# A fixed-point exponential on VectorE and a bias tile in ScalarE's exponentials, in a differential-attention block

## What is computed

```python
scores = jnp.einsum('bhtd,bhsd->bhts', q, k)          # 32 maps of 2048x2048 for each batch
attn_w = jax.nn.softmax(scores.astype(jnp.float32), axis=-1)
aw = attn_w.reshape(Bsz, H, 2, Tt, Tt)
aw = aw[:, :, 0] - lam * aw[:, :, 1]
attn = jnp.einsum('bhts,bhsd->bhtd', aw, v)
```

## Time and profile before

| what | value |
|---|---|
| median of 3 runs | 3668.96 us (3667.09 to 3672.54) |
| time of the profiled execution | 3665.59 us |
| its span, first to last instruction | 3663.9 us |
| mean granted TensorE clock | 0.986 |
| ScalarE busy | 3516.9 us, 96% |
| TensorE busy | 3381.3 us, 92% |
| VectorE busy | 2854.8 us, 78% |
| exponentials on ScalarE | 2732 instructions, 3479.8 us |

### The profile page before, as it was taken

The page is one execution under the profiler, slowest core; times in us unless marked ns, Lnnn a source line. Parts: engine busy times, 40 slices in busy tenths (PEclk is TensorE's granted clock), DMA queues, the critical chain, the costliest instruction groups (busy, mean ns, idle before and its releaser), DMA issues. The chain is left out here.

```text
span 3663.9 us, 74558 instructions
## 1 busy us (share of the span) xinstructions
PE 3381.3 (92%) x30574; PEld 754.8 (21%) x30574; DVE 2854.8 (78%) x4024; ACT 3516.9 (96%) x2808; POOL 449.9 (12%) x283
## 2 busy tenths in 40 slices
PE   8898989999899999999989999999998999989998
PEld 5121111122121121212212112121221111111112
DVE  6688888884598888888368888888747778878876
ACT  4999999999999999999999999999999999999997
POOL 3111101020010111111001110111101001000001
PEclk9999999999999999999999999999999999999999
DMA  6111110111111111111121111111012111000011
GB/s 193 37 27 44 32 36 21 34 43 33 43 39 28 44 50 40 42 29 50 41 48 42 34 36 50 45 42 53 29 35 63 47 36 31 22 27 21 20 27 32
DMA packets 221201, 150.94 MB, mean 41 GB/s; under 512 B 127420, under 2 KB 206220, under 8 KB 220844
## 3 DMA queue, kind: packets, MB, share of 16 engines
q1 hardware_dynamic: 220028, 145.19, 14.9%
q10 hardware_dynamic: 816, 0.79, 0.1%
HBM read 72.50 MB, written 59.19 MB: 36 GB/s over the span
## 5 line engine op out<-in xcount | busy, mean ns | idle before, releaser
L1229 ACT ACTIVATE probs<-ps 128x1536 f32<-128x1536 f32 (+1 forms) x2732 | 3479.8, 1628 | 88.1 <-PE ps L1344 83.1
L1372 PE MATMUL ps<-probs,values 128*32 128x512 f32 x14492 | 2067.4, 610 | 55.5 <-DVE wmod_sb L1721 42.6
L1344 PE MATMUL ps<-queries,keys 25*128 25x512 f16 x7680 | 1008.2, 388 | 184.0 <-ACT probs L1229 161.1
L1344 PEld LDWEIGHTS ps<-queries,keys 25*128 25x128 f16 x7680 | 248.9, 91 | 2024.9 <-ACT probs L1229 1907.6
L1372 PEld LDWEIGHTS ps<-probs,values 128*32 128x32 f32 x14492 | 301.4, 108 | 477.9 <-issue 417.0
L1151 POOL TENSOR_TENSOR seg_rs<-seg_ms,neg_half 128x16 f32<-128x16 f32 x64 | 191.5, 2992 | 1142.0 <-DVE seg_ms L1800 1141.9
L1788 DVE STREAM_TRANSPOSE seg_t<-ps 128x512 f32<-128x512 f32 x127 | 91.0, 717 | 282.3 <-PE ps L1372 281.8
L1717 DVE SCALAR_TENSOR_TENSOR wmod_sb<-wmod_sb 128x1024 f32<-128x1024 f32 x231 | 282.8, 1224 | 5.8
L1699 DVE TENSOR_SCALAR d_y<-ps 128x512 f32<-128x512 f32 x240 | 165.7, 691 | 119.8 <-PE ps L1344 104.9
L1699 DVE TENSOR_SCALAR g_y<-ps 128x512 f32<-128x512 f32 x222 | 153.4, 691 | 120.8 <-PE ps L1344 117.4
L1372 PE MATMUL ps<-wmod_sb,values 128*32 128x512 f32 x868 | 238.7, 630 | 0.0
(11 more groups left out here) (186 smaller groups left out, 1975.2 us busy)
## 6 DMA issues: line engine op xcount, KB each, us to landing
v_scr<-a_v SPq DMA_DIRECT2D x16, 1024.0 KB, 5.0
values<-v_scr SPq DMA_DIRECT2D x29, 512.0 KB
queries<-q_scr SPq DMA_DIRECT2D x116, 96.0 KB
keys<-k_scr SPq DMA_DIRECT2D x116, 96.0 KB
e_x<-in_x_dram SPq DMA_DIRECT2D x18, 512.0 KB, 5.9
attn_scr<-seg_o SPq DMA_DIRECT2D x254, 32.0 KB
e_attn<-attn_scr SPq DMA_DIRECT2D x31, 256.0 KB, 3.7
e_hT<-turned SPq DMA_DIRECT2D x240, 32.0 KB, 2.0
```

What stands on the lines that cost most here:

```text
L1229: nc.scalar.activation(probs[:, s % PRING, at, :], ps[:, base + at.start:base + at.stop:at.step, :], ACT.Exp, scale=1.0 / SQUARE).then_inc ...
L1344: last = nc.tensor.matmul(ps[:, score_bank(n), :], keys[buf][at, u * P:(u + 1) * P], queries[buf][at, tc * CH:(tc + 1) * CH], start=True, ...
L1372: last = nc.tensor.matmul(pv[row:row + VW, :], values[buf][:, n % SEG_BANKS // HEADS, j // 2, :], probs_of(n), start=(i == 0), stop=(i == ...
```

## The change

In `share_part` the seven instructions become six. The score is scaled in `share_read` by log2(e) times 2^23 and written as a 32-bit integer, so that its bits read as a floating-point number hold the whole exponent in the exponent field and the fraction in the mantissa. Two TENSOR_SCALAR instructions with a bitwise AND and an XOR or OR take these two apart, and four SCALAR_TENSOR_TENSOR instructions evaluate a polynomial of degree 6 and multiply. A subtraction (TENSOR_TENSOR) and the rounding and conversion by arithmetic are gone. The blocks of VectorE come out eight times as large as before, and ScalarE's Exp gets a bias of log 8, held in a new tile `eight` of 128x1, so that all exponentials have the same factor. GpSimd writes this tile at the start. The planned costs are those of the six instructions.

```diff
-    D_LINKS = 6
+    D_LINKS = 5
-    SHARE_COST = (695, 1230, 695, 1225, 1225, 1225, 1225)
+    SHARE_COST = (695, 695, 1225, 1225, 1225, 1225)
+            nc.gpsimd.memset(eight[:, :], EIGHT).then_inc(eight_set, 1)
+            act.wait_ge(eight_set, 1)
-                nc.scalar.activation(probs[...], ps[...], ACT.Exp, scale=1.0 / SQUARE).then_inc(exp_done, 1)
+                nc.scalar.activation(probs[...], ps[...], ACT.Exp, bias=eight[:, 0:1], scale=1.0 / SQUARE).then_inc(exp_done, 1)
-                V.tensor_scalar(fractions[j][...], ps[:, score_bank(n), :], EXP_LOW * SQUARE, QUARTER_LOG2E / SQUARE, ALU.max, ALU.mult).then_inc(d_read, 1)
+                V.tensor_scalar(fractions[j][...].bitcast(I32), ps[:, score_bank(n), :], EXP_LOW * SQUARE, LOG2E_BITS / SQUARE, ALU.max, ALU.mult).then_inc(d_read, 1)
                 if part == 0:
-                    link.then(V.tensor_scalar(whole, f, ROUND, -ROUND - SHIFT, ALU.add, ALU.add))
+                    link.then(V.tensor_scalar(whole.bitcast(I32), f.bitcast(I32), WHOLE_BITS, WHOLE_FLIP, ALU.bitwise_and, ALU.bitwise_xor))
                 elif part == 1:
-                    link.then(V.tensor_tensor(f, whole, f, ALU.subtract))
+                    link.then(V.tensor_scalar(f.bitcast(I32), f.bitcast(I32), PART_BITS, PART_SIGN, ALU.bitwise_and, ALU.bitwise_or))
                 elif part == 2:
-                    link.then(V.tensor_scalar(whole.bitcast(mybir.dt.int32), whole, BIAS + SHIFT, 2.0 ** 25, ALU.add, ALU.mult))
+                    link.then(V.scalar_tensor_tensor(f, f, POLY[0], f, ALU.add, ALU.mult))
                 elif part == 3:
-                    link.then(V.scalar_tensor_tensor(out, f, -POLY[0], f, ALU.add, ALU.mult))
+                    link.then(V.scalar_tensor_tensor(out, f, POLY[1], f, ALU.add, ALU.mult))
                 elif part == 4:
-                    link.then(V.scalar_tensor_tensor(out, out, POLY[1], out, ALU.add, ALU.mult))
-                elif part == 5:
                     link.then(V.scalar_tensor_tensor(out, out, POLY[2], f, ALU.add, ALU.mult))
                 else:
-                    V.scalar_tensor_tensor(out, out, -POLY[3], whole, ALU.add, ALU.mult).then_inc(d_done, 1)
+                    V.scalar_tensor_tensor(out, out, POLY[3], whole, ALU.add, ALU.mult).then_inc(d_done, 1)
```

More of the change, by code:

```diff
@@ L14 @@
 F16 = mybir.dt.float16
+I32 = mybir.dt.int32
 P = 128
[L19 to L26, removed]
+POLY = [-0.9341297723814943, 2.4233820625103575, 5.176821583615651, 1.7852414559499343]
+POLY_SCALE = 0.2812099198503226
+EIGHT = float(np.log(8.0))
+WHOLE_BITS, PART_BITS, PART_SIGN = 0x7F800000, 0x007FFFFF, -0x41800000
+WHOLE_FLIP = 0x40000000 | int(np.float32(POLY_SCALE).view(np.int32)) & PART_BITS
+LOG2E_BITS = float(np.log2(np.e) * 2.0 ** 23)
 EXP_LOW = -87.0
@@ L526, in adaln_diff_attention @@
         neg_half = sb("neg_half", [P, 16])
+        eight = sb("eight", [P, 1])
         wq, wk, wv, wo, wf = (sb(f"w_{n}", [P, EC, E]) for n in ("q", "k", "v", "o", "f"))
@@ L671, in adaln_diff_attention @@
         consts_set = sem("consts_set")
+        eight_set = sem("eight_set")
         c_loaded = sem("c_loaded")
@@ L1228, in _ @@
                 at, base = exps_of(s), s % RING * WIDE
-                nc.scalar.activation(probs[:, s % PRING, at, :], ps[:, base + at.start:base + at.stop:at.step, :], ACT.Exp, scale=1.0 / SQUARE).then_inc(exp_done, 1)
+                nc.scalar.activation(probs[:, s % PRING, at, :], ps[:, base + at.start:base + at.stop:at.step, :], ACT.Exp, bias=eight[:, 0:1], scale=1.0 / SQUARE).then_inc(exp_done, 1)
             for h in range(2):
@@ L1698, in share_read @@
                 dve.wait_ge(scores_ready, slot_of(n) + 1)
-                V.tensor_scalar(fractions[j][:, half * CH:(half + 1) * CH], ps[:, score_bank(n), :], EXP_LOW * SQUARE, QUARTER_LOG2E / SQUARE, ALU.max, ALU.mult).then_inc(d_read, 1)
+                V.tensor_scalar(fractions[j][:, half * CH:(half + 1) * CH].bitcast(I32), ps[:, score_bank(n), :], EXP_LOW * SQUARE, LOG2E_BITS / SQUARE, ALU.max, ALU.mult).then_inc(d_read, 1)
             def share_part(share, part):
```

## The result

The changed kernel takes 3829.01 us, the median of four runs (3828.42 to 3830.11), against 3669.74 us before: ratio 1.0434, 95% interval 1.0416 to 1.0452, slower. The profiled execution took 3828.42 us, with a span of 3826.7 us and a mean granted clock of 0.994.

A forecast was written before the change was run, and what follows sets the result against it. ScalarE, 96% busy, was taken as the bound: profiled 3665.6 us + 232 for the bias operand - 67 of idle time given back = 3831, with the median 3.4 us above the profiled execution 3833 us; range 3780 to 3885.

The forecast's parts named there:

- The operand doesn't hide: ScalarE's exponentials: the bias tile lengthens each of 2732 intervals by 0.085 us, 232 us in all (210 to 260).
- The first rival: ScalarE's exponentials: the bias operand's fetch hides, interval stays 1.343 us, price 0; 3602 us, faster; chance 0.14.
- the lead: ScalarE: an exponential's record starts up to 0.43 us before the one before it ends; the fetch might happen there.
- The pages and the rows: Skill page: about 93 ns per 128x1 pointer operand on an ACTIVATE; ScalarE's copies in the profile agree with 90 ns.
- What is given back: ScalarE's idle time from late VectorE blocks: 67 of 72 us come back, bounds 45 and 87.
- ScalarE's own slack: Longer exponential intervals lengthen each 28 us segment by 1.8 us, giving VectorE that much more time.
- The blocks: VectorE's block falls from 7.52 to 6.3 us, bitwise instructions at 0.70 us; 282 us less over 231 blocks.
- the second rival: VectorE stays late, through bitwise forms at 1.22 us or the new order; 20 us come back, 3881 us; chance 0.05.
- The third: ScalarE's exponentials feel only part of the operand, 0.025 to 0.06 us each; 3670 to 3770 us; chance 0.05.
- The batch ends: ScalarE's waits at three batch ends, around a flag's reading: 15 us, nothing to do with blocks, expected to stay.
- the records of Exp would hardly overlap: Sign in the profile after: ScalarE's Exp records overlap by hardly more than 0.1 us, mean length falling to about 1.54 us.
- the choice of 0.085 between 0.077 and 0.095: Operand's cost per exponential interval: 0.077 us if fetched at the start side alone, 0.095 if it adds to all; 0.085 taken.

The follow-up runs named there:

- the constant bias: Changed kernel with the exponentials' bias (log 8) written as a constant of the instruction in place of the 128x1 tile; 3595.17 us, ratio 0.9801 to the kernel before.
- the second operand: Changed kernel with the exponentials' scale also read from a 128x1 tile, same value; 4081.03 us, ratio 1.1122 to the kernel before.
- The kernel with the tile alone: Kernel before, VectorE's seven instructions kept, with only a 128x1 bias tile of zeros added to the exponentials; 3857.87 us, ratio 1.0511 to the kernel before.

## Why the prediction was right

The time was forecast as 3833 us and is 3829. By its steps:

- *The operand doesn't hide.* Right, and shown by the constant bias (234 us back) and the second operand (252 us more). The term was 0.085 us an exponential, 232 us; it measured 0.088, 240 us. It had been read from a few short runs of instructions that have nothing to do with exponentials. The first rival, the lead in which a fetch might fit, fell, though the lead is larger than the 0.43 us that the prediction gives it: by the earlier trace rows the eighth exponential ends at 497.02 - 1.343 = 495.68 and the ninth starts at 495.15, 0.53 us earlier.
- *The pages and the rows.* The Trainium skill ("ScalarE: Activation LUTs", section "What ACT_TABLE_LOAD costs") gives about 93 ns for each pointer operand. The traces agree: 0.088 us for the first operand and 0.090 to 0.092 for the second, as a cost of the interval.
- *What is given back.* 67 us were forecast; idle time fell by 88 - 19 = 69, and the time lost by 75, since 9 of the 97 us lost before were no idle time in the rows. In the argument for it one weight was off: I took ScalarE's own slack (1.8 us a segment) and VectorE's shorter blocks (2.2) as enough together. The kernel with the tile alone shows that the first removes 40 of the 88 us by itself, and the kernel with the constant bias that the second removes 64 by itself. They overlap, since together they remove 69. I also didn't count the plan: the order was treated as a risk only, and it is worth some 22 us at the old pace of ScalarE.
- *The blocks.* Bitwise forms 0.69 us in the rows above (0.71 in the other half of the blocks) against the 0.70 that I took; VectorE busy 2572.5 against 2570. With this and the waits for the last part gone, the second rival fell. The third fell too: no less than the whole operand is felt.
- *The batch ends.* 13.9 us left, 15 forecast. That they have nothing to do with blocks is not right as it was written: what TensorE waits for there is a late read of a bank by VectorE. It is late whatever the length of the blocks, so the size stands.
- *Wrong:* that the records of Exp would hardly overlap and their mean length would fall to 1.54 us. It rose from 1705 to 1920 ns. A record without a backlog is 1.54 us (the one at 82.15 us, behind 0.26 us of idle time), and the starts still run ahead of the ends (1.424 against 1.431), so that the lead builds up to more than half a microsecond as before (the exponential at 545.06 us lasts 1.99, and the next starts at 546.49). I had assumed that the fetch would stop the starts from leading. It slows starts and ends alike, 0.094 and 0.088. That is also why the choice of 0.085 between 0.077 and 0.095 was a little low.

The two errors of size, 8 us too little for the operand and 8 us too little given back, cancelled. That the forecast came within 4 us is luck: by its sizes it was good to some 10 us. What is left is as large as the earlier start of the exponentials, which it didn't have.

## What to carry to other kernels

When one engine is filled to 96% by a few thousand instructions, what counts is the interval between two of them, end to end; read it from a run of them in the timeline, and ask for each operand, not only for each instruction, what it adds. A bias that is the same constant on all partitions belongs in the instruction: here the tile turned a gain of 2.0% into a loss of 4.3%. And a saving on an engine that runs beside the bound is worth no more than the idle time that it causes there; measure it with the rest held still, because a slowdown elsewhere gives part of the same time back: here 40 of the 88 us.

## What the runs showed of the hardware that I had not expected

A nonzero constant bias in these ACTIVATEs with Exp costs nothing that can be seen: 1.344 us against 1.343 with none. The lead of the records grows in a long run of exponentials (starts every 1.330, ends every 1.343; with the operand 1.424 and 1.431), so a mean length of 1.7 or 1.9 us says nothing of the cost of one. Nor does its change: the kernel with the constant has a mean of 1739 ns and the one before 1705, at the same interval. Which stage of ScalarE makes the starts run ahead stays open; no run was made for it.
